# Graph layer on one core: sums ahead of overflow numbers on TensorE, dst comparisons and the mean on ScalarE, zero fills behind the first loads

## The chip, the core and the metric

One core of a Trainium2 chip runs the kernel. It has TensorE (PE, matrix products into PSUM), VectorE (DVE), ScalarE (ACT), GpSimd (POOL, here the issuer of scatters by index) and SyncE (SP, here the issuer of plain transfers), which run on their own and wait for each other by semaphores. The metric is device time in microseconds, lower is better.

## The reference

A message-passing layer on 6250 nodes of 64 features and 206250 edges. The edges are sorted by `dst`; `src` is in no order. For each edge a two-layer perceptron is applied to the normed features of its `dst` node and its own attributes, and the results are averaged over the edges of each `src` node.

```
h = maximum(layernorm(x), 0)
e = relu(concat(h[dst], edge_attr) @ W1.T + b1)        # 206250 x 128
e = relu(e @ W2.T + b2)
summed = segment_sum(e, src, 6250); cnt = segment_sum(1, src, 6250)
agg = summed / maximum(cnt, 1)
out = x + relu(concat(h, agg, u[0]) @ Wa.T + ba) @ Wb.T + bb
```

## The kernel before

Edges come in 403 groups of 512 (four tiles of 128). The main loop is written out step by step: in step `s` each engine does its part of the groups around `s`, in an order fixed by the code.

- **Gather by product.** Edges are sorted by `dst`, so a group's nodes lie in a window of 64 rows of a table `h @ W1` in HBM. For group `g` SyncE loads that window and the weights' half (`L`), the attributes (`regA`, name `R` in the code), and every fourth step the dst row of four groups, as differences from the window's start (`dB`, traced as `dstR`). A comparison of the dst row with the row number (line 1112, VectorE, one per group) writes ones and zeros into the lower half of `R`. One product of TensorE (line 1338) then gives the first layer of 512 edges.
- **Layers.** ScalarE applies the first relu (L913), TensorE the second layer (L1364), on a PSUM bank that ScalarE has filled with the bias (`seed`, L902), ScalarE the second relu (L933).
- **Plain groups** (all even ones and a few at the ends, 211): VectorE compares src numbers within each tile (masks `S`, L1148, four instructions a group), TensorE adds up equal ones (L1354), ScalarE copies the sums (L921), VectorE makes the indices (`idx`, L1156), and GpSimd scatters four tiles with an adding transfer into one of four arrays `sums` in HBM (L811). A scatter waits until the last one into its array has landed, and the first into an array waits until its five zero fills have landed; the arrays take turns, so the first four scatters need all four.
- **Sorted groups** (192, odd ones from 3 to 385): edges are put into 49 bins by src number, with four places a bin and 60 overflow places a tile. VectorE makes digits and permutations (`rank`, `perm`, `over`, `earlier`, L1119 to L1128), TensorE counts ranks (L1382) and the **overflow numbers** (L1388 and L1390) and moves rows into their places (L1316, "bins"), ScalarE copies them (L896) and SyncE stores them in `slots`. Overflow rows of two groups are added with masks of their own (`vS`, L1135; L1396), copied by ScalarE (`vscat`, L944) and scattered by GpSimd (L799).
- **Units.** After each block of 32 sorted groups, 25 units per block add up what lies in the slots: SyncE loads two bins of all groups, VectorE compares (L1181), TensorE adds (L1327, 16 products), VectorE accumulates in SBUF (L1099). In the loop a unit stands in an even step; 25 units fall on 32 pairs of steps.
- **End.** After the last scatter, in 13 chunks: the four arrays are loaded (SyncE, three chunks ahead), VectorE adds them and the accumulated bins (L1194 to L1196), takes 1/count (L1199, L1200) and multiplies (L1203); TensorE transposes and does the last two layers with ScalarE's copies and relu between (L953, L960), VectorE adds x (L1209).
- **Zero fills.** Twenty transfers of 645 KB from a tile of zeros fill `sums`. SyncE issues them in its one order: four early (`ZEARLY`), five before the first table store, two before the last one (`ZMID`), and 1, 2, 3, 3 behind the loads of steps 0 to 3 (`ZAFTER`).

A second branch of the loop, for inputs where a window or a bin is too small, isn't taken with these inputs.

## Time and profile before

| | us |
|---|---|
| median of 3 runs | 1938.61 (1929.67 to 1946.6) |
| the profiled execution itself | 1940.46 |
| its span, first to last instruction | 1938.7 |
| TensorE busy (products; weight loads) | 1731.4; 1477.9 |
| VectorE, ScalarE, GpSimd busy | 1478.6, 1168.1, 1522.5 |
| granted TensorE clock, mean | 0.968 |

How to read it: times are of one execution. A group of instructions is given by line, engine, operation and tiles (out<-in), with its busy time, the mean of one instruction, and the idle time of its engine just ahead of it with what ended most of that. "issue" means the engine waited for nothing that the profile shows. Register and semaphore instructions aren't counted as busy, and TensorE's products are pipelined with modelled ends, so its busy share isn't its load at peak. The stages used below are cut at the first scatter (76.4 us), at the first relu of steps 76 and 386 (366.4 and 1718.8 us), and at the end of the last scatter (1870.4 us).

### The profile page before, as it was taken

The numbers are of one execution on the slowest core, as the hardware profiler recorded it, in microseconds if no ns is written. First come the engines' busy times: TensorE is split into PE (matmuls) and PEld (weight loads), VectorE is DVE, ScalarE is ACT, GpSimd is POOL, SyncE is SP. The second block draws the span as 40 slices with busy tenths as digits, with TensorE's granted clock in tenths as the row PEclk, the third lists the DMA queues.
The fourth block names the chain that finished last, engine by engine and source line by source line (L and its number), as shares of the span: only waits on it lengthen the run. The fifth ranks groups of instructions, "written<-read, shape, count | busy, mean of one in ns | idle before, by whom it ended". The sixth has DMA issues, their size and how long they took to land.

```text
span 1938.7 us, 43590 instructions
## 1 busy us (share of the span) xinstructions
PE 1731.4 (89%) x12472; PEld 1477.9 (76%) x12472; DVE 1478.6 (76%) x5072; ACT 1168.1 (60%) x2542; POOL 1522.5 (79%) x991
## 2 busy tenths in 40 slices
PE   5798887999999998998999999999999999987828
PEld 3576776887888877887887888888888888876715
DVE  8576666787887887888887887878888788857727
ACT  4476666666666665666666666666666666653302
POOL 8388888888888888888888888878888878877840
PEclk9899999999999999999999999999999999989968
DMA  9788888999999999999999999999999999989766
GB/s 351 224 162 158 157 156 151 185 193 189 201 197 188 200 186 195 192 189 189 200 197 193 189 197 198 194 183 195 201 202 197 198 192 190 201 180 226 157 135 190
DMA packets 322283, 372.12 MB, mean 192 GB/s; under 512 B 42592, under 2 KB 203584, under 8 KB 321408
## 3 DMA queue, kind: packets, MB, share of 16 engines
q1 hardware_dynamic: 185856, 306.18, 55.6%
q0 software_dynamic: 135360, 62.15, 34.5%
q8 instruction: 110, 1.80, 0.4%
q10 hardware_dynamic: 832, 0.97, 0.2%
q14 instruction: 125, 1.02, 0.2%
HBM read 203.87 MB, written 159.27 MB: 187 GB/s over the span
## 4 chain that ended last, share of the span: by engine, by line
PE 31%; SPq 17%; DVE 15%; DMA 13%; POOL 13%; issue 9%; ACT 1%; DVEq 0%; POOLq 0%; ACTq 0%
POOL sums L811 12%; DMA regC<-slots 8%; PE bank L1327 8%; PE bank L1316 6%; PE bank L1338 6%; PE bank L1364 6%; SPq L585 4%; DVE regC L1181 4%; DVE regC L1121 3%; DMA sums<-regA,idx 3%; SPq L608 2%; SPq L586 2%; PE bank L1354 2%; SPq L622 2%; SPq L580 2%
## 5 line engine op out<-in xcount | busy, mean ns | idle before, releaser
L811 POOL DMA_INDIRECT sums<-regA,idx x844 | 1328.3, 1574 | 292.0 <-issue 246.2
L913 ACT ACTIVATE h<-bank,b1c 128x512 f32<-128x512 f32 x403 | 276.8, 687 | 406.3 <-PE bank L1338 393.0
L1316 PEld LDWEIGHTS bank<-h,regC 128*128 128x128 f32 x3072 | 390.2, 193 | 134.9 <-ACT h L933 73.5
L1316 PE MATMUL bank<-h,regC 128*128 128x130 f32 x3072 | 413.6, 278 | 31.9 <-ACT h L933 31.9
L1338 PE MATMUL bank<-regA,L 128*128 128x512 f32 x806 | 427.1, 612 | 9.3 <-DVE regA L1112 6.0
L1364 PE MATMUL bank<-w,h 128*128 128x128 f32 x3224 | 429.7, 277 | 0.0
L1364 PEld LDWEIGHTS bank<-w,h 128*128 128x128 f32 x3224 | 396.7, 194 | 1.0 <-issue 1.0
L1327 PE MATMUL bank<-regC 128*128 128x129 f32 x2352 | 308.1, 286 | 24.3 <-DVE regB L1099 17.3
L933 ACT ACTIVATE h<-bank 128x512 f32<-128x512 f32 x403 | 241.5, 599 | 140.8 <-PE bank L1364 138.5
L1181 DVE TENSOR_SCALAR regC<-lows,regC 128x128 f32<-128x128 f32 x1176 | 256.0, 315 | 86.4 <-DMA regC<-slots 64.6
L1327 PEld LDWEIGHTS bank<-regC 128*128 128x128 f32 x2352 | 284.5, 198 | 26.6 <-issue 25.6
L1354 PEld LDWEIGHTS bank<-h,regC 128*128 128x128 f32 x1688 | 223.7, 192 | 101.7 <-issue 100.1
L896 ACT ACTIVATE regC<-bank 128x260 f32<-128x260 f32 x768 | 271.5, 385 | 2.7 <-PE bank L1316 2.4
L1148 DVE TENSOR_SCALAR regC<-src,srcF 128x128 f32<-128x128 uint16 x844 | 207.1, 331 | 83.7 <-DMA src<-rows_src 79.0
L902 ACT ACTIVATE bank<-b2b 128x512 f32<-128x512 f32 x403 | 241.8, 600 | 6.6
L1112 DVE TENSOR_SCALAR regA<-dstR,oh_row 64x512 f32<-64x512 uint8 x403 | 213.8, 531 | 27.9 <-DMA dstR<-rows_dst 15.4
L1354 PE MATMUL bank<-h,regC 128*128 128x130 f32 x1688 | 225.0, 276 | 0.0
L921 ACT ACTIVATE regA<-bank 128x520 f32<-128x520 f32 x211 | 127.7, 605 | 116.4 <-DMA sums<-regA,idx 73.1
L799 POOL DMA_INDIRECT sums<-vscat,vidx x96 | 152.3, 1586 | 52.0 <-issue 24.3
L1121 DVE TENSOR_TENSOR regC<-bank,ranks 128x784 f32<-128x784 f32 x192 | 187.1, 974 | 6.1
L1119 DVE TENSOR_REDUCE rank<-bank 128x4 f32<-128x196 f32 x192 | 69.5, 362 | 132.2 <-PE bank L1382 127.4
L1338 PEld LDWEIGHTS bank<-regA,L 128*128 128x128 f32 x806 | 123.8, 194 | 13.5 <-DVE regA L1112 8.5
(139 smaller groups left out, 1266.4 us busy)
## 6 DMA issues: line engine op xcount, KB each, us to landing
regC<-slots SPq DMA_DIRECT2D x294, 260.0 KB, 4.7
regA<-in_ea SPq DMA_DIRECT2D x202, 256.0 KB
slots<-regC SPq DMA_DIRECT2D x192, 260.0 KB
src<-rows_src SPq DMA_DIRECT2D x107, 256.0 KB
slots<-regC SPq DMA_DIRECT2D x192, 138.1 KB
sums<-regA,idx POOLq DMA_INDIRECT x844
dstR<-rows_dst SPq DMA_DIRECT2D x101, 128.0 KB
sums<-zeros SPq DMA_DIRECT2D x20, 645.0 KB, 7.9
```

The costliest lines, as they stand in the source:

```text
L811: nc.gpsimd.indirect_dma_start(out=sums[k], out_offset=bass.IndirectOffsetOnAxis(ap=idx[:, n % RING, t:t + 1], axis=0), in_=scat[:, n % 4, ...
L896: nc.scalar.activation(slot_sb[:, n % 2, :, t, :], psSlot(t), ACT.Copy).then_inc(slot_ready, 1)
L902: nc.scalar.activation(psL2(g % 2).rearrange("p (t f) -> p t f", t=TPG), b2b[:, :].unsqueeze(1).broadcast_to([P, TPG, H]), ACT.Copy).then_ ...
L913: nc.scalar.activation(h1[:, s % 2, :], psL1(s % 2), ACT.Relu, bias=b1c[:, :]).then_inc(h1_ready, 1)
L933: nc.scalar.activation(h2[:, g % 2, :, 0:H], psL2(g % 2).rearrange("p (t f) -> p t f", t=TPG), ACT.Relu).then_inc(h2_ready, 1)
L1121: VE.tensor_tensor(perm[:, n % 2, :, OVER:PW].rearrange("p t (b j) -> p t b j", j=CAP), ranked.unsqueeze(3).broadcast_to([P, TPG, NBIN, CAP]),
L1181: made = VE.tensor_scalar(oh2[0:rows, m % 2, i, t, :], lows[0:rows, i, :], loaded(m)[0:rows, i, t, C:W], -float(b), ALU.subtract, ALU.is_e ...
L1316: last = T.matmul(psSlot(t)[:, k, :], place, h2[:, g % 2, t, :], start=True, stop=True)
L1327: last = T.matmul(psUnit(m)[:, i * C:(i + 1) * C], oh2[0:rows, m % 2, i, t, :] if not general else zeros[0:rows, 0:LO], loaded(m)[0:rows, ...
L1338: T.matmul(psL1(s % 2), L[:, s % RING, :], R[:, s % RING, :], start=True, stop=True).then_inc(l1_done, 1)
L1354: last = T.matmul(bank[:, 6 + t // 2, (t % 2) * W:(t % 2 + 1) * W], S[:, n % 4, t, :], h2[:, g % 2, t, :], start=True, stop=True)
L1364: last = T.matmul(psL2(g % 2)[:, t * H:(t + 1) * H], h1[:, g % 2, t * TILE:(t + 1) * TILE], w2[:, :], start=False, stop=True, skip_group_c ...
```

## The change

It does five things.

1. In TensorE's step the overflow numbers move behind the overflow sum and the unit.
2. The comparison of the dst row for all groups but the first three goes from VectorE to ScalarE, as two activations: `|dst - row|` (Abs with a bias per partition) and `relu(1 - that)`, with the seed between them. ScalarE does it for group `s + 2` in step `s`, where VectorE did it for `s + 1`; ScalarE so waits for the dst row itself. TensorE and SyncE wait for both kinds.
3. The four masks of a plain group become one instruction on VectorE, with the src row and the src numbers broadcast as its two inputs.
4. The two fills of `ZMID` go, and `ZAFTER` becomes (1, 2, 2, 2, 1, 1, 1, 1).
5. At the end the product with 1/count goes from VectorE to ScalarE, four activations a chunk with a scale per partition, and half of the first three chunks' loads are issued by ScalarE.

```diff
-ZEARLY, ZFIRST, ZMID = 4, 9, 2
-ZAFTER = (1, 2, 3, 3)
+ZEARLY, ZFIRST = 4, 9
+ZAFTER = (1, 2, 2, 2, 1, 1, 1, 1)
...
+def by_act(g):
+    return 2 < g < NG
...
-            for k in range(ZMID):
-                zero(ZFIRST + k)
             store_p(2)
...
-                        wait(sp, oh_ready, GPP * (i - 1))
+                        wait(sp, oh_ready, sum(1 for g in range(GPP * (i - 1)) if not by_act(g)))
+                        wait(sp, oh_act_ready, sum(1 for g in range(GPP * (i - 1)) if by_act(g)))
...
-                    for k in range(NSETS):
+                    for k in range(NSETS if c >= NACC else NSETS // 2):
...
+                g = s + 2
+                if by_act(g):
+                    n, i = g - 3, g // GPP
+                    if n == 0:
+                        act.wait_ge(oh_bias_ready, 1)
+                    act.wait_ge(dB_in[i % 2], 16 * (i // 2 + 1))
+                    wait(act, l1_done, g - RING + 1)
+                    nc.scalar.activation(R[D:P, g % RING, :], dB[D:P, i % 2, g % GPP, :], ACT.Abs, bias=oh_bias[D:P, :]).then_inc(oh_far, 1)
                 if 1 <= s and s + 1 < NG:
                     seed(s + 1)
+                if by_act(g):
+                    act.wait_ge(oh_far, n + 1)
+                    nc.scalar.activation(R[D:P, g % RING, :], R[D:P, g % RING, :], ACT.Relu, bias=1.0, scale=-1.0).then_inc(oh_act_ready, 1)
...
+                    act.wait_ge(rc_ready, c + 1)
+                    wait(act, aggT_psum, c - 1)
+                    for r in range(r1 - r0):
+                        made = nc.scalar.activation(agg[:, c % 2, r, :], s2[:, c % 2, r * C:r * C + H], ACT.Copy, scale=rc[:, c % 2, 1, r:r + 1])
+                    made.then_inc(agg_ready, 1)
...
-                if 0 <= g < NG:
+                if 0 <= g < NG and not by_act(g):
...
-                    for t in range(TPG):
-                        made = VE.tensor_scalar(S[:, n % 4, t, :], sB_of(g)[:, t * TILE:(t + 1) * TILE], srcF[:, TPG * g + t:TPG * g + t + 1], None, ALU.is_equal)
-                    made.then_inc(mask_ready, 1)
+                    VE.tensor_tensor(S[:, n % 4, :, :], sB_of(g).rearrange("p (t e) -> p t e", t=TPG), srcF[:, TPG * g:TPG * (g + 1)].unsqueeze(2).broadcast_to([P, TPG, TILE]),
+                                     ALU.is_equal).then_inc(mask_ready, 1)
...
-                    wait(dve, aggT_psum, c - 1)
-                    VE.tensor_tensor(agg[:, c % 2, 0:m, :], s1v[:, :, 0:H], rc[:, 1, 0:m].unsqueeze(2).broadcast_to([P, m, H]), ALU.mult).then_inc(agg_ready, 1)
-                    dve.wait_ge(agg_ready, c + 1)
```

TensorE, an even step with a unit and the start of the odd step behind it, in the middle of the loop. Before (L1338 first layer, L1354 sums of a plain group, L1364 second layer, L1388 and L1390 overflow numbers, L1327 half of the unit's 16 products as written):

```order
L1338 MATMUL bank<-regA,L 128x512
L1354 MATMUL bank<-h,regC 128x130 x4
L1364 MATMUL bank<-w,h 128x128 x4
L1388 MATMUL bank<-over,prefix 128x4
L1390 MATMUL bank<-earlier,onesb 128x4
L1327 MATMUL bank<-regC 128x129 x8
L1338 MATMUL bank<-regA,L 128x512
```

With the change the same instructions are L1370, L1386, L1396, L1429, L1431 and L1358:

```order
L1370 MATMUL bank<-regA,L 128x512
L1386 MATMUL bank<-h,regC 128x130 x4
L1396 MATMUL bank<-w,h 128x128 x4
L1358 MATMUL bank<-regC 128x129 x8
L1429 MATMUL bank<-over,prefix 128x4
L1431 MATMUL bank<-earlier,onesb 128x4
L1370 MATMUL bank<-regA,L 128x512
```

The unit has moved ahead of the two overflow products.

ScalarE, an even and an odd step in the loop. Before (L913 first relu, L921 copy of plain sums, L929 keys, L933 second relu, L902 seed, L896 copies of bins):

```order
L913 ACTIVATE h<-bank,b1c 128x512
L921 ACTIVATE regA<-bank 128x520
L929 ACTIVATE h<-srcF 128x4
L933 ACTIVATE h<-bank 128x4x128
L902 ACTIVATE bank<-b2b 128x512
L913 ACTIVATE h<-bank,b1c 128x512
L896 ACTIVATE regC<-bank 128x2x130 x2
L933 ACTIVATE h<-bank 128x4x128
L896 ACTIVATE regC<-bank 128x2x130 x2
L902 ACTIVATE bank<-b2b 128x512
```

With the change (L923, L931, L939, L943, L912, L906 in the same order; L954 and L959 are the two new activations):

```order
L923 ACTIVATE h<-bank,b1c 128x512
L931 ACTIVATE regA<-bank 128x520
L939 ACTIVATE h<-srcF 128x4
L943 ACTIVATE h<-bank 128x4x128
L954 ACTIVATE regA<-dstR,oh_bias 64x512
L912 ACTIVATE bank<-b2b 128x512
L959 ACTIVATE regA<-regA 64x512
L923 ACTIVATE h<-bank,b1c 128x512
L906 ACTIVATE regC<-bank 128x2x130 x2
L943 ACTIVATE h<-bank 128x4x128
L906 ACTIVATE regC<-bank 128x2x130 x2
L954 ACTIVATE regA<-dstR,oh_bias 64x512
```

Two activations a step have come in, on either side of the seed.

## Rows read from the trace of the kernel before

**Rows 1.** Costliest groups of the page: busy us, mean ns | idle before, releaser.
```profile
L811 POOL DMA_INDIRECT sums<-regA,idx x844 | 1328.3, 1574 | 292.0 <-issue 246.2
...
L1112 DVE TENSOR_SCALAR regA<-dstR,oh_row 64x512 f32<-64x512 uint8 x403 | 213.8, 531 | 27.9 <-DMA dstR<-rows_dst 15.4
...
L799 POOL DMA_INDIRECT sums<-vscat,vidx x96 | 152.3, 1586 | 52.0 <-issue 24.3
```

**Rows 2.** Windows: stage, its us, busy us (count) by engine, clock, DMA share, GB/s.
```profile
core 0: us, PE busy (x) PEld busy (x) DVE busy (x) ACT busy (x) POOL busy (x), PEclk, DMA share, GB/s
0.00:76.40 76.40, 45.94 (x204) 29.88 (x205) 52.42 (x97) 31.45 (x54) 41.97 (x51) 0.86 0.91 327
76.40:366.40 290.00, 257.42 (x1775) 212.21 (x1774) 197.24 (x659) 198.73 (x448) 242.76 (x156) 0.97 0.85 158
366.40:1718.80 1352.40, 1281.23 (x9533) 1113.25 (x9532) 1098.54 (x3884) 877.44 (x1938) 1114.87 (x706) 0.99 0.95 194
1718.80:1870.40 151.60, 103.14 (x761) 91.45 (x759) 80.45 (x344) 44.42 (x78) 122.92 (x79) 0.92 0.79 159
```

**Rows 3.** Waits of GpSimd, whole span: us in total, times, longest us.
```profile
POOL sums L799 <- ACT vscat L944: 21.1, 9, 3.9
```

**Rows 4.** Waits of TensorE between 200 and 1700 us, the same columns.
```profile
PE bank L1388 <- DVE vS L1135: 54.1, 41, 3.1
...
PE bank L1388 <- DVE over L1125: 11.6, 18, 2.4
```

**Rows 5.** Timeline of ScalarE: start us, us, instruction, [idle before <-releaser].
```profile
505.24 0.69 ACT L913 ACTIVATE h<-bank,b1c 128x512 f32<-128x512 f32 x1 [1.55 <-PE bank L1338]
505.83 0.69 ACT L896 ACTIVATE regC<-bank 128x260 f32<-128x260 f32 x2
507.09 0.60 ACT L933 ACTIVATE h<-bank 128x512 f32<-128x512 f32 x1 [0.56 <-PE bank L1364]
...
509.11 0.69 ACT L913 ACTIVATE h<-bank,b1c 128x512 f32<-128x512 f32 x1 [0.31 <-PE bank L1338]
510.01 0.60 ACT L921 ACTIVATE regA<-bank 128x520 f32<-128x520 f32 x1 [0.20 <-PE bank L1354]
...
510.90 0.60 ACT L933 ACTIVATE h<-bank 128x512 f32<-128x512 f32 x1 [0.19 <-PE bank L1364]
...
513.68 0.69 ACT L913 ACTIVATE h<-bank,b1c 128x512 f32<-128x512 f32 x1 [1.55 <-PE bank L1338]
```

**Rows 6.** Timeline of TensorE over the same pair of steps.
```profile
504.18 1.02 PE L1338 MATMUL bank<-regA,L 128*128 128x512 f32 x2
...
510.75 2.03 PE L1327 MATMUL bank<-regC 128*128 128x129 f32 x16
512.62 1.02 PE L1338 MATMUL bank<-regA,L 128*128 128x512 f32 x2
```

**Rows 7.** Timelines of GpSimd and of VectorE around 911 us.
```profile
911.16 4.67 POOL L811 DMA_INDIRECT sums<-regA,idx  x1 [0.30 <-issue]
...
910.93 3.48 DVE L1185 TENSOR_TENSOR x_sb<-x_sb,bbb 128x3200 f32<-128x3200 f32 x1
```

**Rows 8.** The start: timelines of SyncE's queue, VectorE, GpSimd; landing of the fills (L527).
```profile
72.83 1.70 SPq L586 DMA_DIRECT2D L<-p_table  x2
73.40 0.49 DVE L1112 TENSOR_SCALAR regA<-dstR,oh_row 64x512 f32<-64x512 uint8 x1 [6.53 <-DMA dstR<-rows_dst]
...
76.41 1.80 POOL L811 DMA_INDIRECT sums<-regA,idx  x1 [30.62 <-DVE idx L1156]
...
82.23 1.55 POOL L811 DMA_INDIRECT sums<-regA,idx  x1 [0.30 <-issue]
...
DMA to landing us min/median/max: 5.0/7.9/17.6
```

**Rows 9.** Timeline of VectorE at the end: one chunk and the next one's start.
```profile
1912.30 1.22 DVE L1194 TENSOR_TENSOR regC<-regA 128x1032 f32<-128x1032 f32 x1
...
1915.43 0.69 DVE L1203 TENSOR_TENSOR regC<-regC,rc 128x512 f32<-128x512 f32 x1
...
1916.50 1.22 DVE L1194 TENSOR_TENSOR regC<-regA 128x1032 f32<-128x1032 f32 x1
```

More of the change, by code:

```diff
@@ L31 @@
 ZQ = 5
-ZEARLY, ZFIRST, ZMID = 4, 9, 2
-ZAFTER = (1, 2, 3, 3)
+ZEARLY, ZFIRST = 4, 9
+ZAFTER = (1, 2, 2, 2, 1, 1, 1, 1)
 EPS = 1e-5
-assert ZFIRST + ZMID + sum(ZAFTER) == ZQ * NSETS and NG <= P * GPP and N + P < NROWS and N + WIN <= NROWS
+assert ZFIRST + sum(ZAFTER) == ZQ * NSETS and NG <= P * GPP and N + P < NROWS and N + WIN <= NROWS
 def chunk_rows(c0, c1):
@@ L118, in scatter_table @@
         if closes(s - VLAG):
-            table[s - VLAG, 0] = n % NSETS, used[n % NSETS]
-            used[n % NSETS] += 1
+            k = n % NSETS
+            table[s - VLAG, 0] = k, used[k]
+            used[k] += 1
             n += 1
@@ L123, in scatter_table @@
             for t in range(TPG):
-                table[s, t] = n % NSETS, used[n % NSETS]
-                used[n % NSETS] += 1
+                k = n % NSETS
+                table[s, t] = k, used[k]
+                used[k] += 1
                 n += 1
@@ L282, in build @@
         take = parts()
-        s2 = take(KC)
+        s2 = take(2 * KC).rearrange("p (s c) -> p s c", s=2)
         s1 = take(2 * KC).rearrange("p (k c) -> p k c", k=2)
@@ L340, in build @@
         oh_row = sb("oh_row", [P, 1], f32)
+        oh_bias = sb("oh_bias", [P, 1], f32)
         scrapc = sb("scrapc", [P, 1], f32)
@@ L359, in build @@
         mode = sb("mode", [1, 1], i32)
[L361 removed]
+        rc = sb("rc", [P, 2, 2, RCH], f32)
         bank = ctx.enter_context(nc.psum_tensor("bank", [P, 8, 512], f32))
@@ L435, in build @@
         oh_ready = sem("oh_ready")
+        oh_act_ready = sem("oh_act_ready")
+        oh_far = sem("oh_far")
+        oh_bias_ready = sem("oh_bias_ready")
         mask_ready = sem("mask_ready")
@@ L490, in build @@
         agg_ready = sem("agg_ready")
+        rc_ready = sem("rc_ready")
         aggT_psum = sem("aggT_psum")
@@ L594, in _ @@
                         for k in range(sum(ZAFTER[:s]), sum(ZAFTER[:s + 1])):
-                            zero(ZFIRST + ZMID + k)
+                            zero(ZFIRST + k)
                 if is_sorted(s - QLAG):
@@ L944, in _ @@
                     nc.scalar.activation(vscat[:, j % 4, :], psVsum, ACT.Copy).then_inc(vscat_ready, 1)
+            for k in range(NSETS):
+                act.wait_ge(added[k], 16 * SCATTERS[k])
+            for c in range(NACC):
+                r0, r1 = kept_rows(c, c + 1)
+                for k in range(NSETS // 2, NSETS):
+                    act.dma_start(SA[:, c, k, 0:(r1 - r0) * C], sums[k][0:NKEPT, :].rearrange("(p r) c -> p (r c)", p=P)[:, r0 * C:r1 * C]).then_inc(acc_in[c], 16)
             for c in range(NCH + 2):
                 if c < NCH:
+                    r0, r1 = kept_rows(c, c + 1)
+                    act.wait_ge(rc_ready, c + 1)
[3 more added lines that the diff above has]
+                    made.then_inc(agg_ready, 1)
                     act.wait_ge(aggT_psum, c + 1)
@@ L1194, in _ @@
                     link(VE.tensor_tensor(s1[:, :, 0:m * C], SA[:, s, 0:2, 0:m * C], SA[:, s, 2:4, 0:m * C], ALU.add))
[L1195 to L1196 removed]
+                    wait(dve, agg_ready, c - 1)
+                    link(VE.tensor_tensor(s2[:, c % 2, 0:m * C], s1[:, 0, 0:m * C], s1[:, 1, 0:m * C], ALU.add))
+                    VE.tensor_tensor(s2[:, c % 2, 0:m * C], s2[:, c % 2, 0:m * C], acc[:, r0:r1, :].rearrange("p r c -> p (r c)"), ALU.add).then_inc(s2_done, 1)
                     dve.wait_ge(s2_done, c + 1)
[L1198 to L1204 removed]
+                    counts = s2[:, c % 2, 0:m * C].rearrange("p (r c) -> p r c", c=C)[:, :, H]
+                    link(VE.tensor_scalar(rc[:, c % 2, 0, 0:m], counts, 1.0, None, ALU.max))
+                    VE.reciprocal(rc[:, c % 2, 1, 0:m], rc[:, c % 2, 0, 0:m]).then_inc(rc_ready, 1)
                 if c >= 3:
@@ L1332, in step @@
                 if s < NG:
-                    pe.wait_ge(oh_ready, s + 1)
+                    pe.wait_ge(oh_ready, sum(1 for g in range(s + 1) if not by_act(g)))
+                    wait(pe, oh_act_ready, sum(1 for g in range(s + 1) if by_act(g)))
                     pe.wait_ge(ea_in[(s // 2) % 4], 16 * (s // RING + 1))
@@ L1382, in step @@
                     T.matmul(psRank, prefix[:, :], A[:, n % 2, :, :].rearrange("p t b -> p (t b)"), start=True, stop=True).then_inc(rank_done, 1)
-                if is_sorted(s + 1):
-                    n = BINNED_NO[s + 1]
-                    pe.wait_ge(over_ready, n + 1)
-                    pe.wait_ge(perm_ready, n + 1)
-                    free_row(s)
-                    T.matmul(psOver, prefix[:, :], over[:, n % 2, TPG - 1:2 * TPG - 1], start=True, stop=False)
-                    pe.wait_ge(earlier_ready, n + 1)
-                    T.matmul(psOver, onesb[:, :], earlier[:, n % 2, :], start=False, stop=True).then_inc(over_done, 1)
                 if closes(s - VSUM):
@@ L1399, in step @@
                     add_up(k, q, general)
+                if is_sorted(s + 1):
+                    n = BINNED_NO[s + 1]
+                    pe.wait_ge(over_ready, n + 1)
+                    pe.wait_ge(perm_ready, n + 1)
+                    free_row(s)
+                    T.matmul(psOver, prefix[:, :], over[:, n % 2, TPG - 1:2 * TPG - 1], start=True, stop=False)
+                    pe.wait_ge(earlier_ready, n + 1)
+                    T.matmul(psOver, onesb[:, :], earlier[:, n % 2, :], start=False, stop=True).then_inc(over_done, 1)
             general = pe.value_load(mode[0:1, 0:1], min_val=0, max_val=1)
```

7 lines of the change are left out of this document (1 added, 6 removed).

## Prediction

> **What bounds the kernel now.** I read the costliest groups first. TensorE (PE) looks like the bound by busy share, but a modelled busy share says little; GpSimd (POOL) is the one to count. It issues 940 scatters, 844 on L811 and 96 on L799, of 1.574 and 1.586 us, and the 292.0 + 52.0 us of idle time in front of them is mostly "issue" [rows 1]. Rows of the timeline show what that is: 0.30 us stand in front of a scatter even where nothing is waited for [rows 7, 8]. So a scatter costs POOL 1.575 + 0.30 = 1.875 us.
>
> By stage [rows 2], POOL's busy time plus 0.30 us per scatter is 242.8 + 46.8 = 289.6 of 290.0 us from 76.4 to 366.4 us, 1114.9 + 211.8 = 1326.7 of 1352.4 us up to 1718.8, and 122.9 + 23.7 = 146.6 of 151.6 us up to 1870.4. The reader is to see that POOL is full from its first scatter to its last: of its 344.0 us of idle time, 30.6 us are the wait for the first index [rows 8] and 282 us are the fixed 0.30; some **31.7 us** are left as waits that something else causes. Of these, 21.1 us (nine waits) are L799 waiting for ScalarE's `vscat` [rows 3].
>
> TensorE is close behind. A pair of steps (even and odd) with a unit takes it 512.62 - 504.18 = **8.44 us**, of which the unit is 512.62 - 510.75 = 1.87 [rows 6]. POOL needs 4.5 scatters for a pair (four for the plain group, one for every second sorted group): 4.5 x 1.875 = **8.44 us** too. A block has 25 units on 32 pairs, so TensorE without a stall needs 8.44 - 0.22 x 1.87 = 8.03 us on average. Between 366.4 and 1718.8 us (310 steps, 155 pairs) a pair took 8.72: TensorE lost time, and POOL lived on groups that were queued for it. From 200 to 1700 us TensorE's wait ahead of the overflow numbers (L1388) was 54.1 + 11.6 = 65.7 us [rows 4], 0.4 us a pair.
>
> **Part by part.** *TensorE order.* The unit now stands ahead of the overflow numbers, so VectorE's `over` and `vS` get 1.87 us more before TensorE asks for them. The 65.7 us should nearly go in steps with a unit. VectorE's next step, which starts with the overflow slots, begins those 1.87 us later; its comparison of 0.53 us a step (L1112 [rows 1]) is gone, 1.1 us a pair, and its masks get shorter, so I price this at nothing; if that cover went, the next rank would be late and TensorE's bins with it. But TensorE isn't what ends the loop: the gain can only come out where POOL waits, 31.7 us at most.
>
> *Comparisons on ScalarE.* In a pair ScalarE now idles 0.56 + 0.31 + 0.20 + 0.19 + 1.55 = 2.81 of 8.44 us [rows 5], so it works 5.6, and 5.8 with the `vscat` copy of every second pair. Each step gets two 64x512 activations. Nearest row: the biased 128x512 relu takes 0.69 us, and the next instruction begins 0.59 us after it began (505.24 to 505.83). Two per step make 2.36 us a pair: 8.2 of 8.44. In the odd step only the 0.31 us at its end can take them up, so the even step's relu starts some 0.9 us late (more behind a `vscat` copy); the even step has 1.94 us against 1.18 and wins nearly all of it back. In the 22% of pairs without a unit the even step is 1.87 us shorter, and TensorE's second pair of bins then waits some 1.1 us for ScalarE: those pairs take 8.44 - 1.87 + 1.1 = 7.7, and TensorE's mean becomes 0.78 x 8.44 + 0.22 x 7.7 = 8.28 us against POOL's 8.44. The margin shrinks from 0.41 to 0.16 us a pair (25 us in the 155 pairs), while the stalls of 0.4 us a pair mostly go. So I take back 13 of the 31.7 us; ends: -27 (all but landing waits), +10 (ScalarE, which now also waits for the dst row's load in its own queue, with the seed and the next relu behind it).
>
> *VectorE against POOL.* At 910.93 a two-input instruction of 3.48 us ran on VectorE, and the scatter that began at 911.16 took 4.67 us where an undisturbed one takes 1.55 [rows 7, 8]: POOL stood until VectorE was done. All such holding is small: 844 x (1.574 - 1.55) + 96 x (1.586 - 1.55) = 24 us, the excess of the mean over an undisturbed scatter [rows 1]. The comparisons leave VectorE (0.53 us each, 214 us in all); as a share of it I give them 7 us. The four masks of a plain group become one instruction of two SBUF inputs, 128x512, nearest row 0.69 us [rows 9]; 211 of them meet the start of 211 x 0.69 / 1.9 = 77 scatters, and if each lost half of it that is 27 us; I take 10 because the start of a scatter needs the port only in part. Net **+3**, ends -15 and +25. The Trainium skill (SBUF — State Buffer, Who interferes with whom) says a tensor_tensor with two SBUF inputs takes only the shared read interface, and infers that descriptor generation, which writes, isn't held by it. The 4.67 us scatter in this trace speaks against that; by the skill the masks would cost POOL nothing, the term would be -7 and the sum 10 us lower.
>
> *Zeros.* Two zero fills leave the place ahead of the last table store, and before step 4's loads there are 7 + 9 instead of 9 + 2 + 9 of them. One is 0.66 MB, 2.0 us at the 327 GB/s of the start [rows 2]. The first index waited for a mask and, before it, 6.53 us for the dst row of step 4 [rows 8]; those loads stand behind 8 us less of zeros, so the first scatter could come up to 8 us earlier. But each of the first four scatters needs a whole set of zeros, and the last fill is now issued behind step 7's load (before, that load was out by 74.5 us [rows 8]; 4 us earlier with the two fills gone, so about 70.5). A fill lands 5.0 to 7.9 us later, the shortest and the median, so at 75.5 to 78.4; the fourth scatter began at 82.23 [rows 8]. I take **-4.5**; ends -8 and +2. ScalarE's wait for step 4's dst row in its own queue is inside that.
>
> *The end.* After the last scatter VectorE sets a 4.20 us beat per chunk (1912.30 to 1916.50), 0.69 of it the product with 1/count [rows 9] and 0.04 the gap to it. It goes to ScalarE as four 128x128 activations. VectorE's beat becomes 3.47. A quarter-width activation lies between 0.17 and 0.69 us (a quarter of the relu, and the whole); at 0.3 the four are 1.2 us, and with ScalarE's two wide ones a chunk it works 2.6 us of the beat, so I take 3.5 us. Eight chunks run at full clock with VectorE as bound: 8 x 0.7 = 5.6; the first chunk's loads on two queues save under 1. I take **-6**; ends -8 and -2.
>
> **Sum.** -4.5 - 13 + 3 - 6 = -20.5. The profiled execution took 1940.5 us itself: 1920.0. It lies 1.85 us above the median of the runs, so against that median the forecast is **1918 us**.
>
> **Rivals.**
> *ScalarE becomes the bound (slower).* Place: the seed between the two new activations and the relu behind them. If the small overlaps fail, or the dst row's load is late in ScalarE's queue, a pair rises above 8.44. The two stages from 76.4 to 1718.8 us took 1642.4 us for 192 pairs; slower by 1% needs 27 us more there beside the -10.5 of the ends and the +3, so it decides from (1642.4 + 27) / 192 = 8.70 us a pair. At 8.8 they take 1690: the time is 1920.0 + 13 + 47 - 1.9 = 1978. For it: 8.2 of 8.44 is already used. Against: the even step's 1.55 us of idle. The Trainium skill (ScalarE: Activation LUTs, Rules for kernel authors) puts relu, add and multiply on VectorE rather than ScalarE; by that rule the move is a loss, two activations for one instruction.
> *POOL gains nothing in the loop.* The waits for `vscat` stay because ScalarE's copy now stands behind the second activation, and the masks hold scatters: -5 + 12 instead of -13 + 3 gives 1935. For it: POOL is full now whatever TensorE does.
> *Everything comes off.* All but the landing waits go (-27), the port gets freer (-10), -6 and -8 at the ends: 1940.5 - 51 - 1.9 = 1888.
>
> **How the numbers follow.** Forecast 0.60 (its own range 1906 to 1930), ScalarE as bound 0.15, no gain in the loop 0.15, everything 0.10. A measurement here tells about 1% from no change: 1919 and 1958 us. The forecast lies on the first line, 0.35 below it and 0.25 above. Faster: 0.35 + 0.10 = 0.45; same: 0.25 + 0.15 = 0.40; slower: 0.15. The range of 1894 to 1946 leaves out ScalarE as bound and half of the last case, 0.20.
>
> **What would show it.** POOL: 940 scatters with the first at 68 to 73 us; idle beyond 0.30 us each falling from 31.7 to under 20; mean scatter 1.56 to 1.60. TensorE: hardly a wait at the overflow matmul. ScalarE: activations of 0.6 to 0.7 us on 64x512 and busy over 80% from 366 to 1719 us. The end: a beat of 3.4 to 3.7 us. It is wrong if POOL shows idle time in front of L811 with ScalarE or the dst row as releaser.

## The result, and the profile after

The changed kernel is slower: 1944.18 us median of 20 runs (1931.10 to 1956.18) against 1935.02 us of 20 runs of the kernel before (1919.06 to 1946.60). The ratio is **1.0053**, 95% interval 1.0029 to 1.0077, so 6 to 15 us more: inside the forecast range of 1894 to 1946 us, but on the other side of no change than the forecast of 1918. The profiled execution took 1943.8 us.

The groups of the page that answer to [rows 1] (busy us, mean ns | idle before, releaser), with the two new activations and the wide mask:

```profile
L821 POOL DMA_INDIRECT sums<-regA,idx x844 | 1327.2, 1573 | 287.1 <-issue 248.1
...
L954 ACT ACTIVATE regA<-dstR,oh_bias 64x512 f32<-64x512 uint8 x400 | 286.8, 717 | 26.6 <-DMA dstR<-rows_dst 16.8
...
L959 ACT ACTIVATE regA<-regA 64x512 f32<-64x512 f32 x400 | 250.8, 627 | 9.8
...
L809 POOL DMA_INDIRECT sums<-vscat,vidx x96 | 155.4, 1618 | 63.6 <-ACT vscat L965 28.0
...
L1182 DVE TENSOR_TENSOR regC<-src,srcF 128x512 f32<-128x512 uint16 x211 | 143.9, 682 | 65.4 <-DMA src<-rows_src 65.1
```

Two sums are read from such rows for every run below. *Held*: GpSimd's busy time over 1.545 us a scatter (the undisturbed one). Here 1327.2 + 155.4 - 940 x 1.545 = 30.3 us; before 28.3. *Waited*: its idle time, less the wait for the first index and 0.30 us a scatter. Here 287.1 + 63.6 - 22.7 - 282 = 46.0 us; before 31.4 (the prediction's 31.7, whose subtraction is off by 0.3). The two grew by 2.0 and 14.6 us. With -6.8 us at the start and -6.6 at the end (below) that makes +3.2 us, and the two profiled executions differ by 3.4. The waits for ScalarE stand ahead of the overflow scatter L809, as in [rows 3] for the kernel before:

```profile
POOL sums L809 <- ACT vscat L965: 28.0, 23, 2.8
...
POOL sums L809 <- ACT regA L931: 10.2, 14, 1.8
```

The stages, cut at the same events as in [rows 2] (first scatter, first relu of steps 76 and 386, end of the last scatter):

```profile
core 0: us, PE busy (x) PEld busy (x) DVE busy (x) ACT busy (x) POOL busy (x), PEclk, DMA share, GB/s
0.00:69.64 69.64, 43.67 (x201) 28.60 (x201) 49.44 (x84) 31.60 (x55) 43.10 (x52) 0.83 0.93 332
69.64:382.14 312.50, 263.04 (x1789) 208.02 (x1788) 145.01 (x483) 301.34 (x598) 258.24 (x163) 0.99 0.82 156
382.14:1728.58 1346.44, 1289.96 (x9535) 1107.79 (x9533) 865.33 (x3101) 1286.47 (x2558) 1101.07 (x698) 1.00 0.94 194
1728.58:1880.28 151.70, 106.16 (x745) 92.96 (x744) 67.08 (x283) 63.56 (x107) 123.28 (x79) 0.89 0.80 160
1880.28:1942.00 61.72, 39.91 (x207) 28.04 (x207) 41.07 (x78) 31.04 (x75) 0.00 (x0) 0.82 0.71 238
```

By stage against before: the first scatter comes 6.8 us earlier; the steps up to 76, where no unit runs yet, take **22.5 us longer** (312.5 against 290.0, with 163 instructions of GpSimd instead of 156); the middle takes 6.0 less (with 698 of them instead of 706); the last steps are equal; the end is 6.6 shorter (61.7 against 68.3). ScalarE was 69% and 65% busy in the two long stages and is 96% busy now.

The edges of these stages are relus of ScalarE, so part of the 22.5 us is work of GpSimd that now comes before step 76 instead of behind it. GpSimd's idle time beyond 0.30 us an instruction went from 0.4 to 5.4 us ahead of step 76 (312.50 - 258.24 - 163 x 0.30) and from 25.7 to 36.0 us in the middle: it is nearly full ahead of the units in both kernels, and waits later.

ScalarE's waits between the first scatter and step 76, in the kernel before (us in total, times, longest):

```profile
ACT regA L921 <- DMA sums<-regA,idx: 44.6, 20, 6.1
ACT h L933 <- PE bank L1364: 22.2, 50, 1.4
ACT h L913 <- PE bank L1338: 12.9, 19, 5.1
```

There ScalarE stood until scatters had landed: GpSimd set the pace. In the changed kernel the same view, from 69.64 to 382.14 us, has no row at all: ScalarE waits for nobody in 312 us, and it sets the pace of the steps. TensorE's waits between 200 and 1700 us agree; the overflow matmul of [rows 4] is gone from them, and ScalarE has taken its place:

```profile
PE bank L1347 <- ACT regC L906: 60.6, 64, 2.0
PE bank L1347 <- ACT h L943: 22.9, 52, 0.6
```

### The profile page after: what moved, and what is told of

It reads as the page before. It is cut to its first block, busy times and chain, and to the rows that moved or that the text cites. A ratio compares the mean times of both kernels' runs of the same rounds, so it can differ in the third digit from the quotient of the medians.

```text
span 1942.0 us, 43493 instructions
## 1 busy us (share of the span) xinstructions
PE 1742.7 (90%) x12472; PEld 1465.4 (75%) x12472; DVE 1167.9 (60%) x4027; ACT 1714.0 (88%) x3391; POOL 1525.7 (79%) x991
## 4 chain that ended last, share of the span: by engine, by line
POOL 49%; issue 17%; PE 12%; DMA 10%; ACT 4%; SPq 4%; DVE 3%; POOLq 0%; ACTq 0%; DVEq 0%
POOL sums L821 43%; DMA sums<-regA,idx 8%; POOL sums L809 6%; PE bank L1358 3%; PE bank L1347 2%; PE bank L1370 2%; PE bank L1396 2%; ACT regA L959 1%; PE bank L1386 1%; SPq L595 1%; DVE regC L1215 1%; ACT regA L954 1%; SPq L596 1%; DMA regC<-slots 1%; SPq L632 1%
## 5 line engine op out<-in xcount | busy, mean ns | idle before, releaser
L821 POOL DMA_INDIRECT sums<-regA,idx x844 | 1327.2, 1573 | 287.1 <-issue 248.1
L1347 PEld LDWEIGHTS bank<-h,regC 128*128 128x128 f32 x3072 | 382.1, 190 | 244.4 <-ACT regC L906 100.0
L1347 PE MATMUL bank<-h,regC 128*128 128x130 f32 x3072 | 427.6, 282 | 105.6 <-ACT regC L906 75.9
L1370 PE MATMUL bank<-regA,L 128*128 128x512 f32 x806 | 433.4, 620 | 4.6 <-ACT regA L959 2.6
L1396 PE MATMUL bank<-w,h 128*128 128x128 f32 x3224 | 425.8, 275 | 0.0
L1396 PEld LDWEIGHTS bank<-w,h 128*128 128x128 f32 x3224 | 392.6, 192 | 1.1 <-ACT h L923 0.6
L923 ACT ACTIVATE h<-bank,b1c 128x512 f32<-128x512 f32 x403 | 277.1, 688 | 53.9 <-PE bank L1370 44.1
L954 ACT ACTIVATE regA<-dstR,oh_bias 64x512 f32<-64x512 uint8 x400 | 286.8, 717 | 26.6 <-DMA dstR<-rows_dst 16.8
L1358 PE MATMUL bank<-regC 128*128 128x129 f32 x2352 | 295.9, 279 | 16.0 <-issue 7.7
L1386 PEld LDWEIGHTS bank<-h,regC 128*128 128x128 f32 x1688 | 223.2, 192 | 105.0 <-issue 98.1
L1358 PEld LDWEIGHTS bank<-regC 128*128 128x128 f32 x2352 | 276.6, 193 | 19.8 <-issue 17.0
L906 ACT ACTIVATE regC<-bank 128x260 f32<-128x260 f32 x768 | 273.3, 386 | 12.1
L959 ACT ACTIVATE regA<-regA 64x512 f32<-64x512 f32 x400 | 250.8, 627 | 9.8
L943 ACT ACTIVATE h<-bank 128x512 f32<-128x512 f32 x403 | 242.3, 601 | 12.0 <-PE bank L1396 5.5
L912 ACT ACTIVATE bank<-b2b 128x512 f32<-128x512 f32 x403 | 242.6, 602 | 9.8
L1386 PE MATMUL bank<-h,regC 128*128 128x130 f32 x1688 | 225.3, 276 | 2.2 <-ACT h L943 2.2
L809 POOL DMA_INDIRECT sums<-vscat,vidx x96 | 155.4, 1618 | 63.6 <-ACT vscat L965 28.0
L1140 DVE TENSOR_TENSOR regC<-bank,overs 128x240 f32<-128x240 f32 x192 | 77.5, 404 | 208.6 <-PE bank L1431 208.6
L1182 DVE TENSOR_TENSOR regC<-src,srcF 128x512 f32<-128x512 uint16 x211 | 143.9, 682 | 65.4 <-DMA src<-rows_src 65.1
```

Of the source, the lines that this page charges most:

```text
L809: nc.gpsimd.indirect_dma_start(out=sums[k], out_offset=bass.IndirectOffsetOnAxis(ap=vidx[:, j % 6:j % 6 + 1], axis=0), in_=vscat[:, j % 4, ...
L821: nc.gpsimd.indirect_dma_start(out=sums[k], out_offset=bass.IndirectOffsetOnAxis(ap=idx[:, n % RING, t:t + 1], axis=0), in_=scat[:, n % 4, ...
L906: nc.scalar.activation(slot_sb[:, n % 2, :, t, :], psSlot(t), ACT.Copy).then_inc(slot_ready, 1)
L923: nc.scalar.activation(h1[:, s % 2, :], psL1(s % 2), ACT.Relu, bias=b1c[:, :]).then_inc(h1_ready, 1)
L954: nc.scalar.activation(R[D:P, g % RING, :], dB[D:P, i % 2, g % GPP, :], ACT.Abs, bias=oh_bias[D:P, :]).then_inc(oh_far, 1)
L959: nc.scalar.activation(R[D:P, g % RING, :], R[D:P, g % RING, :], ACT.Relu, bias=1.0, scale=-1.0).then_inc(oh_act_ready, 1)
```

## What a pair of steps costs ScalarE

The row pattern that decides the case is a pair of steps *without* a unit. Steps 136 and 137 in the timeline of ScalarE, in the kernel before (start us, us, instruction):

```profile
627.29 0.69 ACT L913 ACTIVATE h<-bank,b1c 128x512 f32<-128x512 f32 x1 [0.31 <-PE bank L1338]
...
633.95 0.69 ACT L913 ACTIVATE h<-bank,b1c 128x512 f32<-128x512 f32 x1
```

The same two steps in the changed kernel:

```profile
640.43 0.69 ACT L923 ACTIVATE h<-bank,b1c 128x512 f32<-128x512 f32 x1
...
642.22 0.72 ACT L954 ACTIVATE regA<-dstR,oh_bias 64x512 f32<-64x512 uint8 x1
642.96 0.60 ACT L912 ACTIVATE bank<-b2b 128x512 f32<-128x512 f32 x1
643.59 0.63 ACT L959 ACTIVATE regA<-regA 64x512 f32<-64x512 f32 x1
644.24 0.69 ACT L923 ACTIVATE h<-bank,b1c 128x512 f32<-128x512 f32 x1
...
648.89 0.28 ACT L965 ACTIVATE vscat<-bank 128x129 f32<-128x129 f32 x1
649.19 0.69 ACT L923 ACTIVATE h<-bank,b1c 128x512 f32<-128x512 f32 x1
```

Before, such a pair took 633.95 - 627.29 = 6.66 us; now it takes 649.19 - 640.43 = 8.76, back to back. A new activation occupies 0.74 us (642.22 to 642.96) or 0.65 us (643.59 to 644.24), so the two cost 1.39 us a step and 2.78 us a pair. A pair without a `vscat` copy takes 8.46 us and one with it 8.76, whether it has a unit or not: 8.61 on average. GpSimd could do with 8.44, and before, 30 of the 155 pairs in the middle took less than 6.8 us and made up for 54 pairs of 9 to 13.2 us (from one L913 row to the next but one). Now no pair takes less than 8.4 and 140 of the 155 take 8.46 or 8.76 within 0.05. The mean over the middle is no longer for that: 1346.44 / 155 = 8.69 us against 8.72.

## Experiments

Theories: **A**, ScalarE sets the pace; **B**, the wide mask or the later overflow numbers cost the time and ScalarE only looks busy. Ratios are against the kernel before, run on the same chip beside them (median about 1932 us there).

**All comparisons back on VectorE**, the rest changed.

```
 def by_act(g):
-    return 2 < g < NG
+    return False
```

> The changed kernel with the dst comparisons of all groups back on VectorE; order, masks, zeros and end stay changed. Theory A (ScalarE sets the pace): in the changed kernel ScalarE has next to no idle time from 69.6 to 1728.6 us and needs 8.61 us per pair of steps (498.03 to 506.49 without a vscat copy, 506.49 to 515.25 with one), and GpSimd waits 14.7 us more than before. Without the two activations ScalarE needs 5.8 us per pair, GpSimd is full again, and the 6.8 us of the start and 6.6 us of the end remain: 1935 - 13.4 = 1922 us, or down to 1910 if the order of the overflow numbers also takes waits away. Theory B (the wide mask on VectorE or the later overflow numbers cost the time, ScalarE only looks busy): 1940 to 1946 us.

Measured 1928.55 us, 0.9978 (0.9957 to 0.9999). The comparisons' place is worth 14 to 15 us of the changed kernel (1.0053 - 0.9978 = 0.75%): A in its direction, though the time lies between the two theories' ranges. Scatters were held for 45.2 us here and GpSimd waited 17.3.

**Half of them back**: `2 < g < NG and g % 2 == 0`.

> The changed kernel with ScalarE making the comparisons of the even groups only, VectorE those of the odd ones. Theory A: ScalarE needs 8.61 - 1.39 = 7.2 us per pair and is no longer the bound: 1908 to 1922 us, as with all comparisons on VectorE or a little below. Theory B: 1940 to 1946 us.

1934.27 us, 1.0006 (0.9980 to 1.0032): neither theory's number. ScalarE needs 7.2 us a pair here, and the kernel looks slower than with no comparison there (0.9978), but the intervals overlap.

**The comparisons alone on ScalarE**, in the kernel before (the edits of part 2 of the change).

> The kernel before with the comparisons of all groups but the first three on ScalarE and nothing else changed. Theory A: the pace is ScalarE's 8.61 us per pair, and the start and the end bring nothing: 1935 + 15 = 1950 us, 1945 to 1958. Theory B: 1932 to 1938 us, as before.

1949.66 us, 1.0095 (1.0073 to 1.0117), 18 us: A. GpSimd's two groups show what was gained and what was lost:

```profile
L820 POOL DMA_INDIRECT sums<-regA,idx x844 | 1315.7, 1559 | 292.6 <-issue 249.9
...
L808 POOL DMA_INDIRECT sums<-vscat,vidx x96 | 148.7, 1549 | 78.8 <-ACT vscat L964 50.7
```

Held 12.1 instead of 28.3 us, as VectorE's comparison no longer stands beside a scatter; waited 59.1 instead of 31.4. The 16 us won on the held time are real, and the waits grew by more.

**One more activation per plain group** in the changed kernel, which nothing reads.

```
+                if is_plain(g):
+                    wait(act, pad_done, sum(1 for k in range(2, g) if is_plain(k)))
+                    nc.scalar.activation(pad[:, :], srcF[:, 0:P], ACT.Copy).then_inc(pad_done, 1)
                 if 1 <= s and s + 1 < NG:
                     seed(s + 1)
```

> The changed kernel with one more activation on ScalarE for each plain group from group 2 on, a 128x128 copy that nothing reads, ahead of the seed; some 0.30 us from one start to the next by the nearest row (the vscat copy, 270.08 to 270.38). Theory A: every one of the about 190 of them up to 1729 us lengthens the loop by nearly its whole 0.30 us: 1944 + 45 to 57 = 1989 to 2001 us. Theory B: ScalarE has room, 1944 to 1950 us.

1967.21 us, 1.0183 (1.0156 to 1.0210), 1.30% or 25 us over the changed kernel: half of what A said. The copy displaced the seed by 0.22 us, not 0.30. The windows of the two long stages:

```profile
68.87:388.00 319.13, 261.75 (x1788) 206.88 (x1788) 144.41 (x484) 307.99 (x633) 258.60 (x164) 1.00 0.80 153
388.00:1752.40 1364.40, 1299.90 (x9535) 1109.77 (x9534) 856.53 (x3102) 1318.44 (x2715) 1111.93 (x698) 1.00 0.92 192
```

Ahead of the units 6.6 us more for some 36 copies, 0.18 of the 0.22 each; in the middle 18.0 for 155, 0.12 each. By these edges ScalarE sets the pace of the steps nearly alone ahead of the units, and about by half in the middle.

Four runs then took the parts apart. Theory **C**: held and waited add up over the parts; rival **D**: what one loses less the other loses more.

**Narrow masks, comparisons on VectorE** (order, fills and end stay changed): the first experiment with the four `tensor_scalar` of before.

> The changed kernel with all comparisons back on VectorE and the masks again as four instructions; order, zeros and end stay changed. Theory C (the terms add up on GpSimd): a scatter's time over 1.545 us, summed over the 940, was 28.2 us before, 12.2 with the comparisons alone on ScalarE, 30.3 in the changed kernel, 45.2 with the comparisons back on VectorE: so the comparisons on VectorE hold scatters for 15 to 16 us and the wide masks for 15 to 18 more than the narrow. GpSimd's waits over 0.305 us were 27.4, 55.0, 42.0 and 13.2: the order takes 14 us away. So here 28 + 13: 1928.5 - 17 = 1911 us, 1907 to 1917. Rival D (something else supplies the middle of the loop at its own pace, since 310 steps there took 1352, 1344, 1346 and 1347 us in the four kernels, so what scatters lose less GpSimd waits more): 1925 to 1931 us, with the waits up by some 15.

1919.68 us, 0.9932 (0.9906 to 0.9957), **the fastest of all**: some 13 us under the kernel before. The wide masks cost 9 us beside comparisons on VectorE (0.9978 - 0.9932 = 0.46%), about half of what C said. GpSimd's groups:

```profile
L821 POOL DMA_INDIRECT sums<-regA,idx x844 | 1324.1, 1569 | 295.6 <-issue 239.5
...
L809 POOL DMA_INDIRECT sums<-vscat,vidx x96 | 150.0, 1563 | 42.4 <-issue 27.3
```

Held 21.8 instead of 45.2 us, waited 32.5 instead of 17.3: the waits rose by the 15 us of D, the held time fell by more.

**Narrow masks, even groups on ScalarE.**

> The changed kernel with the comparisons of even groups on ScalarE, odd on VectorE, and the masks as four instructions. Theory C: scatters held 36.4 - 17 = 19 us, waits as with the wide masks, 24: 1934 - 17 = 1917 us, 1910 to 1921. Rival D: 1930 to 1937 us.

1927.66 us, 0.9968 (0.9941 to 0.9996): held only 15.8 us, waited 43.2, and some 7 us slower than without ScalarE's half. Against the half version with wide masks it is 7 us of the 17 that C said, between the two theories' ranges.

**The order alone**, in the kernel before: the overflow block moved behind the units.

> The kernel before with the overflow numbers behind the unit on TensorE and nothing else changed. Theory C: GpSimd's waits over 0.305 us fall from 27.4 to 13, scatters stay held for 28: 1933.5 - 14 = 1920 us, 1915 to 1925. Rival D: 1930 to 1936 us.

1932.52 us, 1.0005 (0.9978 to 1.0031): D, nothing that can be told. TensorE's waits between 200 and 1700 us did change as meant, against 54.1 and 11.6 in [rows 4], but 22 us of idle time ahead of the units (L1327) and of the overflow rows' keys (L1375) came in their place:

```profile
PE bank L1397 <- DVE vS L1135: 25.1, 41, 0.9
PE bank L1327 <- issue: 12.9, 23, 1.1
PE bank L1375 <- issue: 9.2, 12, 1.7
...
PE bank L1397 <- DVE over L1125: 0.3, 1, 0.3
```

**The wide masks alone**, in the kernel before.

> The kernel before with the masks of a plain group as one instruction and nothing else changed. Theory C: scatters held 28 + 17 = 45 us; what GpSimd waits (27) shrinks by a few us as it is later: 1933.5 + 13 = 1946 us, 1941 to 1952. Rival D: 1931 to 1937 us.

1943.01 us, 1.0059 (1.0034 to 1.0083), 11 us: C by the time. The profiled execution doesn't show the loss: it was the fastest of the twelve, 1935.59 us, and held 41.7 us but waited only 15.7, together less than before (28.3 and 31.4). How a mask holds a scatter, in the changed kernel, timelines of GpSimd and of VectorE:

```profile
148.59 1.55 POOL L821 DMA_INDIRECT sums<-regA,idx  x1 [0.30 <-issue]
150.60 1.96 POOL L809 DMA_INDIRECT sums<-vscat,vidx  x1 [0.46 <-issue]
...
150.47 0.68 DVE L1182 TENSOR_TENSOR regC<-src,srcF 128x512 f32<-128x512 uint16 x1
```

The mask began 0.13 us ahead of the scatter, which took 0.41 us longer. In that trace of the changed kernel 77 scatters began beside a mask and were held for 22.3 us together, 0.29 each; the narrow masks of the kernel before held theirs for 1.2 us.

**Wide masks undone beside comparisons on ScalarE.** The changed kernel with the narrow masks.

> The changed kernel with the masks as four instructions and all comparisons still on ScalarE. If the masks cost as much as beside comparisons on VectorE (8.9 us between 1919.7 and 1928.5; 22.3 us of scatter time in the trace of the changed kernel stand at scatters that began beside a wide mask): 1944 - 9 = 1935 us, 1931 to 1938. If ScalarE sets the pace everywhere, what the scatters get back is waited for: 1941 to 1946 us.

1940.27 us, 1.0047 (1.0026 to 1.0068), against 1.0053 with the wide ones: no difference that can be told. GpSimd's groups:

```profile
L821 POOL DMA_INDIRECT sums<-regA,idx x844 | 1314.9, 1558 | 290.3 <-issue 247.8
...
L809 POOL DMA_INDIRECT sums<-vscat,vidx x96 | 149.1, 1553 | 79.9 <-ACT vscat L965 49.9
```

Held 11.7 and waited 64.8 us, 76.5 together; in the changed kernel 30.3 and 46.0, 76.3 together. What the scatters got back, GpSimd waited for. So in the changed kernel the wide masks cost nothing that can be told, and the comparisons on ScalarE cost 1.0047 - 0.9932 = 1.15%, **22 us**.

**Start and end alone**: the kernel before with the fills' order and the mean on ScalarE.

> The kernel before with the order of the zero fills and the end with ScalarE alone; overflow numbers, comparisons and masks as before. The order alone gave a ratio of 1.0005; in traces the first scatter came 6.8 us earlier with 1.5 to 3 us of waits for fills given back, and the stretch from the last scatter to the end was 6.6 us shorter. So 1933.5 - 11.5 = 1922 us, 1918 to 1926, if the parts add up; 1928 to 1934 if the loop takes the start's gain back.

1921.18 us, 0.9957 (0.9930 to 0.9983): the parts add up here. Beside the fastest run (0.9932) the order may bring a few us; the intervals overlap.

Where is it lost? Theory **E**: ahead of the units only; **F**: in the middle as well.

**Comparisons on ScalarE from group 76 on only**: `76 <= g < NG`.

> The changed kernel with the comparisons on ScalarE only from group 76 on, VectorE making the first 76. Theory E (the loss is made ahead of the units): up to step 76 no step has a unit, TensorE and VectorE could go faster than ScalarE's 8.61 us per pair, and step 76 comes at 382.1 us in the changed kernel and at 366.4 with all comparisons on VectorE; from there to step 386 both take the same, 1346.4 and 1347.1. So here 1928.5 us, as with all on VectorE, 1924 to 1933. Theory F (ScalarE loses as much in the middle, where it is also without idle time, and the lead of the first steps is used up there): 1936 to 1945 us.

1933.41 us, 1.0022 (1.0003 to 1.0041), between the two: 0.31% or 6 us under the changed kernel, 0.44% over all on VectorE.

**Up to group 75 only**: `2 < g < 76`.

> The changed kernel with the comparisons on ScalarE only for groups 3 to 75, on VectorE from group 76 on. With them only from 76 on it took 1933.4 us, 11 less than the changed kernel and 5 more than with all on VectorE (1928.5). If the two halves add up: 1928.5 + 11 = 1939 us, 1935 to 1943. If the first steps' loss is caught up later by a middle that isn't paced by ScalarE: 1927 to 1932 us.

1937.02 us, 1.0034 (1.0013 to 1.0056), 0.56% over all on VectorE. So the 73 groups ahead of the units cost 0.56% and the 327 behind them 0.44%; together 1.0%, where both at once cost 0.75%: both parts of the loop lose, and neither theory alone has it. E is also wrong about where GpSimd loses the time. Windows of the two long stages, all comparisons on VectorE and then groups 3 to 75 on ScalarE:

```profile
69.01:366.40 297.39, 257.33 (x1761) 213.84 (x1761) 191.11 (x550) 197.52 (x445) 246.30 (x155) 0.94 0.84 159
366.40:1713.50 1347.10, 1285.87 (x9533) 1105.41 (x9532) 1061.37 (x3414) 872.53 (x1938) 1126.46 (x707) 1.00 0.93 194
...
69.12:378.67 309.55, 259.68 (x1776) 205.41 (x1777) 143.76 (x479) 297.25 (x591) 258.56 (x162) 1.00 0.83 157
378.67:1723.04 1344.37, 1286.09 (x9532) 1106.01 (x9531) 1064.45 (x3415) 877.53 (x1939) 1114.28 (x700) 1.00 0.93 194
```

GpSimd's idle time beyond 0.30 us an instruction is 4.6 and 8.5 us in the first, 2.4 and 20.1 in the second: what the early comparisons cost is waited for in the middle, where those comparisons are no longer on ScalarE. The likely reason, not tested by itself, is that the early steps build up a lead over GpSimd, which is smaller then and is missed later.

Why does half of the comparisons (with narrow masks) cost time, though ScalarE has room? Theory **G**: the dst row's load is late in its queue. In that version ScalarE's waits between 380 and 1700 us held

```profile
ACT regA L954 <- DMA dstR<-rows_dst: 47.4, 42, 4.3
```

**The load two steps earlier**, beside half of the comparisons and narrow masks.

```
-                    if s % GPP == 0:
-                        i = s // GPP
+                    if s in (0, GPP) or s % GPP == 2 and s // GPP >= 1 and s + 2 < NG:
+                        i = (s + 2) // GPP if s % GPP == 2 else s // GPP
```

> The changed kernel with narrow masks, the comparisons of even groups on ScalarE, and the dst row's load issued two steps earlier in SyncE's order from the third load on. Without the earlier load this took 1927.7 us, 8 more than with all comparisons on VectorE (1919.7), though ScalarE needs only 7.2 us a pair there. Theory G (the load is late in ScalarE's queue: it waited 42 times, 47.4 us in all, up to 4.3, between 380 and 1700 us, and TensorE then waited 47.2 us for ScalarE's copies of the bins): the waits go, and it takes 1912 to 1920 us. Rival (ScalarE's longer even steps themselves delay TensorE): 1925 to 1930 us.

1934.78 us, 1.0019 (0.9997 to 1.0042). The row is gone from ScalarE's waits, and the time went up, not down.

**The earlier load with all comparisons on VectorE**, narrow masks.

> The changed kernel with narrow masks and all comparisons on VectorE (1919.7 us), with the dst row's load issued two steps earlier in SyncE's order. If the earlier load itself costs (SyncE then waits for comparisons two steps nearer to it, and what it issues behind that comes later): 1924 to 1930 us. If not: 1917 to 1923 us, and the earlier load did nothing for the half version because the waits it took away were not what cost time.

1934.75 us, 1.0021 (0.9995 to 1.0048): the earlier load itself costs 0.89%, 17 us, and half of the comparisons beside it nothing more. So the run before it doesn't refute G: with the waits for the row gone, the half on ScalarE cost nothing. It doesn't show G either, since the earlier load's own cost may hide that of the half. VectorE's waits between 380 and 1700 us for the slots' loads were 78.1 us in the fastest version and are

```profile
DVE regC L1216 <- DMA regC<-slots: 108.1, 92, 4.2
```

here: what SyncE issues behind the earlier load comes later. That this alone makes the 17 us wasn't tested.

**Late comparisons, narrow masks, earlier load**, all three together.

> The changed kernel with narrow masks, the comparisons on ScalarE only from group 76 on, and the dst row's load two steps earlier. Theory E: the first steps keep their pace, and from then on no comparison holds a scatter (some 12 us): 1919.7 - 8 = 1912 us, 1905 to 1917. Theory F: ScalarE's 8.61 us a pair against GpSimd's 8.44 cost up to 0.17 x 155 = 26 us in the middle, less the lead and the 12: 1920 to 1932 us.

1940.01 us, 1.0033 (1.0004 to 1.0062): slower than E and F both said. With the earlier load in it, it can't be told from that load's cost.

**Idle work on ScalarE in the fastest version.** Theory **H**: ScalarE's in-order work costs by itself where it isn't full; **I**: it doesn't. Two copies in every even step, where the half version had its two comparisons.

```
+                if 2 < g < NG and g % 2 == 0:
+                    wait(act, pad_done, g - 4)
+                    nc.scalar.activation(pad[D:P, :], srcF[D:P, 0:512], ACT.Copy).then_inc(pad_done, 1)
                 if 1 <= s and s + 1 < NG:
                     seed(s + 1)
+                if 2 < g < NG and g % 2 == 0:
+                    act.wait_ge(pad_done, g - 3)
+                    nc.scalar.activation(pad[D:P, :], srcF[D:P, 0:512], ACT.Copy).then_inc(pad_done, 1)
```

> The changed kernel with narrow masks and all comparisons on VectorE (1919.7 us), and in every even step from the second on two further activations on ScalarE, 64x512 copies that nothing reads, where the two comparison activations of an even group stood; some 1.25 us a pair. Theory H (ScalarE's in-order work as such costs: what stands behind the two, the seed and the next relu, comes later, and TensorE with it, though ScalarE is not full): 1924 to 1930 us, as with half of the comparisons. Theory I (the load is free where ScalarE is not full, and what cost time in the half version was tied to the data: the dst row's load and the place of its issue): 1917 to 1923 us.

1927.34 us, 0.9969 (0.9945 to 0.9992), as the half version's 0.9968: for H, though its interval and that of the fastest version (up to 0.9957) still touch. Steps 136 and 137, ScalarE's timeline:

```profile
622.65 0.69 ACT L925 ACTIVATE h<-bank,b1c 128x512 f32<-128x512 f32 x1 [0.31 <-PE bank L1379]
...
625.06 0.63 ACT L959 ACTIVATE pad<-srcF 64x512 bf16<-64x512 f32 x1
...
626.34 0.63 ACT L964 ACTIVATE pad<-srcF 64x512 bf16<-64x512 f32 x1
...
630.40 0.69 ACT L925 ACTIVATE h<-bank,b1c 128x512 f32<-128x512 f32 x1
```

The unit-free pair takes 7.75 us instead of 6.66 (7.84 in the half version). A mean of 7.2 us a pair says that ScalarE has room; but the room lies in pairs with a unit, and the pairs that catch up are ScalarE's. That these 1.1 us are what costs the time isn't shown, and the trace speaks against it: this execution took 1921.4 us, the profiled one of the fastest version 1921.1, the stretch ahead of the units took 294.1 against 292.3 us, and the middle is as long in both. The middle of the fastest version, and of this one:

```profile
361.80:1705.10 1343.30, 1282.52 (x9532) 1105.44 (x9531) 1096.39 (x3880) 874.65 (x1939) 1108.52 (x706) 1.00 0.94 195
...
363.06:1706.26 1343.20, 1282.55 (x9532) 1105.36 (x9531) 1100.56 (x3883) 1074.39 (x2249) 1105.18 (x705) 1.00 0.94 195
```

So what the half version pays for stays open.

## Why the prediction was wrong

**The start was right.** The first scatter came 6.8 us earlier and the fourth waited for its fill:

```profile
69.64 1.80 POOL L821 DMA_INDIRECT sums<-regA,idx  x1 [22.72 <-DVE idx L1190]
...
77.37 1.54 POOL L821 DMA_INDIRECT sums<-regA,idx  x1 [2.21 <-DMA sums<-zeros]
```

It began at 77.37 (forecast 75.5 to 78.4) against 82.23, so -4.9 us for the -4.5 of the sum. ScalarE's idle time for the dst row's load is in front of L954, 16.8 us in all: half of it ahead of the first scatter, as the sum supposed, none in the 312 us behind that, and 8.4 us (11 times) in the middle.

**The end was right.** 6.6 us for 6. VectorE's beat and ScalarE's four products:

```profile
1903.89 1.22 DVE L1228 TENSOR_TENSOR regC<-regA 128x1032 f32<-128x1032 f32 x1
...
1907.24 1.22 DVE L1228 TENSOR_TENSOR regC<-regA 128x1032 f32<-128x1032 f32 x1
...
1907.03 1.28 ACT L980 ACTIVATE regC<-regC,rc 128x128 f32<-128x128 f32 x4 [0.28 <-DVE rc L1235]
```

This beat is 3.35 us, and the eight up to the last chunk are 3.6 on average, of 3.35 to 3.85 (forecast 3.5); the four take 1.28 us (forecast 1.2).

**The port: the sum near, by luck; both parts too small.** Forecast -7 and +10. Measured on the held time: -16 with the comparisons alone (28.3 to 12.1), +13 with the masks alone (28.3 to 41.7), +2 with both. 77 scatters beside a mask is the number worked out, but each lost 0.29 us, near the half mask (27 us in all) that the prediction had set aside; it took 10 us, 0.13 each, "because the start of a scatter needs the port only in part". The Trainium skill (SBUF — State Buffer, Who interferes with whom) infers that a `tensor_tensor` doesn't hold descriptor generation; taken for these scatters, that would have had the masks cost nothing. The 1.96 us scatter beside the mask speaks against it as the 4.67 us of [rows 7] did.

**The order: nothing.** The waits at the overflow matmul went, as forecast; the 13 us that were to come out of the loop with them did not (-4 to +6 us by the interval of the order alone).

**ScalarE: the step that failed.** The term is the -13: 13 of GpSimd's 31.7 us of waits were to go, and they grew by 14.6 instead. The other terms held: -6.8 at the start (with 2.2 us of fill waits counted among the waits), +2.0 at the port, -6.6 at the end. Behind the -13 stands the price of ScalarE. The prediction priced the two activations at 2.36 us a pair, by the 0.59 us between the relu and the next instruction. That row is a relu out of PSUM with another instruction out of PSUM behind it; 64x512 activations out of SBUF stand 0.74 and 0.65 us apart, 2.78 a pair. ScalarE so needs 8.46 and 8.76 us, not 8.2 of 8.44. The larger error stands behind it: "those pairs take 7.7", the pairs without a unit. Only TensorE's wait of 1.1 us was added there, as if ScalarE were free in a pair without a unit; its work is the same with and without one, and even the 8.2 of the prediction's own sum is more than 7.7. So a pair's mean was not 8.28 but, by ScalarE's need, 8.61, over GpSimd's 8.44. And the 36 pairs ahead of step 76, which have no unit at all, were left out of that mean; the comparisons of the groups up to 75 alone cost 0.56%.

The prediction's own sign of being wrong, idle time in front of the plain scatter with ScalarE as releaser, hardly came (2.4 us): the waits are those of L809 for `vscat` (28.0 us, 21.1 before) and for the sums' copy (10.2, 3.6 before). That `vscat` would be late behind the second activation is what the rival "POOL gains nothing in the loop" named.

The case is nearest to the rival "ScalarE becomes the bound", at a price below the 8.8 it was given: (1728.58 - 69.64) / 192 = 8.64 us a pair. By the prediction's own formula the two stages then take 8.64 x 192 - 1642.4 = 16.5 us more; with that in place of -13 and +3 the sum is -4.5 + 16.5 - 6 = +6, and 1940.5 + 6 - 1.9 = 1944.6 us, where 1944.18 was measured. As the 8.64 is read from the changed kernel itself, this is an account and no second proof; the proof is the 22 us between the two runs with narrow masks, comparisons on ScalarE or on VectorE. The Trainium skill (ScalarE: Activation LUTs, Rules for kernel authors) puts relu, add and multiply on VectorE; the 22 us that the comparisons cost on ScalarE agree with it here.
